# Feeding the first tile's raw weight pieces and the gated and last weights by converting transfers, with the raw copies moved beside the second layer's products

## The chip, the cores and the metric

The kernel runs on one core of a Trainium2 chip. The metric is device time in microseconds, lower is better. The profile shown is of one execution; the times are of three others.

## What is computed

The reference takes x of 8 x 1024 rows of 256 (8192 rows), normalises each row, and computes two things from it: a random-feature product `s` (256 features, exponentials, times a 256x256 matrix) and a ternary feed-forward net `g`. The output is `x + s * g`. Cut to the part that fills the time:

```python
h = silu(xn @ w1.T * w1_s) * (xn @ w2.T * w2_s)   # w1, w2: 1024 x 256, entries -1, 0, 1
h = gelu(h @ h1.T * h1_s)                          # h1: 1024 x 1024
h = gelu(h @ h2.T * h2_s)                          # h2: 1024 x 1024
g = silu(h @ w3.T * w3_s)                          # w3: 256 x 1024
out = x + s * g
```

## The kernel before

**Tiling.** T is 512 rows, a half; a tile is two halves, and there are NT = 8 tiles. A tile goes through: the gated layer (`gated`, `gated_step`, L331) for each half, the feature products (`dots`, `mix`), the two 1024x1024 layers (`product_layer`, L713), and the last layer (`down`, L780). Everything for TensorE is in fp32r. Each activation is split into a high and a low part (`split`, one conversion on ScalarE and one subtraction on VectorE), and each product is run for both parts.

**The fast scheme.** A 1024x1024 layer on a tile is a 2x2 block product done in seven products in place of eight (`FAST`, L32): with the raw weight blocks A11, A12 and A22 and with the sums S2, S1, S3 and S4 of blocks. The order in a layer is A11, A12, S2, S1, S3, S4, A22. Each of the seven is four groups m of 32/4 = 8 matmuls (four pieces k, high and low), so 32 matmuls; a layer is 224 matmuls on 28 pieces. A piece is 128x512 floats, 256 KB. Below, a product is numbered by w = 0 to 6 in its layer.

**The ring.** The pieces go through a ring of eight buffers (`RING`), in the order of `pieces` (L391), 56 a tile. `ring_step` (L416) waits for a piece, uses it, and at m = 3 marks the buffer free and calls `feed` (L397), which sends the piece eight places further on. So the four pieces of product w + 2 are sent while the last group of product w runs, and product w + 1 (32 matmuls) is the time they have to land. In the kernel before, the first eight pieces come straight from the weights by POOL's queue, which converts them to fp32r; all the others are sent by SP out of `hs`, a DRAM copy in which the raw blocks and the sums stand side by side, bit for bit. SP works through its waits and sends in the order written: a feed that waits for a sum to be stored holds all feeds behind it.

**The factory.** `factory` (L492) fills `hs`, on POOL. For each of eight (layer, k) it loads four raw blocks (two transfers of 512 KB, `load`), makes four sums with four tensor_tensor instructions (`make`), and stores them (1 MB). The buffers are borrowed from tiles that are needed later: `use` gives which, among them `quad[0]` (the third round), which VectorE must have back for its first sum t1, and F (`early`). `load(n)` waits until the last store out of its buffer has landed. Between its rounds the factory also sends `copy_raw` (L481), DRAM to DRAM copies of 1 MB that put a raw block of one layer into `hs`, six in all:

```python
            make(2)
            load(5)
            make(3)
            copy_raw(pool, 0, ["A22"])
            make(4)
            load(6)
            copy_raw(pool, 1, ["A11"])
```

`load(5)` stands ahead of `make(3)` and waits for the second round's store. After the factory POOL counts the weights' entries that are not -1, 0 or 1 (`count_good`, L551), with loads of 128 KB into `seen`; the count is read in the last tile.

**The start.** SP sends x of the first half, the column scales, proj, win, four transfers of w1 and w2 (halves, into `quad[1]` and `quad[4]`), x of the second half (L468 to L479). ScalarE converts w1 and w2 to fp32r (`round_w`, L590), for which matmuls of `gated_step` wait (`w12_ready`). The factory's first loads wait for all four w1/w2 transfers (L522).

**The norms.** `norms_out` (L314) stores 512 floats, one by one, from a 128x4 tile to DRAM (`q_h<-sm`); `norms_in` waits for them and reads them back as a row.

**w3.** It goes by SP from its array to a rearranged DRAM copy `w3d` (L897) and from there into `w3` (L932); `down` needs it at the end of the first tile.

**x of the next tile.** `load_x` for the next two halves stands between `dots` and `mix` (L900), ahead of SP's stores of s; their statistics are `fill` tasks in products 2 and 3 of the first layer.

Of the kernel before, what the change touches and what calls it, by code (L numbers as in the profile page):

```python
# [5 lines left out]
P = 128  # L6
D = 256
H = 1024
R = 256
T = 512  # L10
NB = T // P
KD = D // P
KH = H // P
Q = KH // 2
# [9 lines left out]
RING = 8  # L24
# [69 lines left out]
def build(nc, x, win, proj, cols_in, w3s_in, wT, out):  # L94
# [3 lines left out]
    with ExitStack() as ctx:  # L98
# [57 lines left out]
        q_h = nc.dram_tensor("q_h", [NH, NB, P], F32).ap()  # L156
        w3d = nc.dram_tensor("w3d", [P, KH * D], F32).ap()
        s_h = nc.dram_tensor("s_h", [NH, P, NB, D], F32).ap()
# [8 lines left out]
        def port(name):  # L167
            return Port(sem(name))
# [5 lines left out]
        d_first = [port(f"d_first{i}") for i in range(RING)]  # L174
        d_w3d = port("d_w3d")
        d_land = [port(f"d_land{i}") for i in range(5)]
# [18 lines left out]
        def cast(dst, src, *tokens, func=ACT.Identity, scale=1.0):  # L195
            act.wait(*tokens)
            return act.mark(lambda e: e.activation(dst, src, func, scale=scale))  # L197
# [48 lines left out]
        def load_x(h):  # L246
            sp.wait(*xin_free[h % 2])
            return d_x[h % 2].send(sp, xin[h % 2][:, :, :], x_h[h])
# [76 lines left out]

        w_round = {}

        def w12_ready(m):
            return [w_round[n, m // Q] for n in range(2)]

# [60 lines left out]
        pieces = [(layer, name, k) for _ in range(NT) for layer in range(2) for name, _ in FAST for k in range(Q)]  # L391
        fed = [0]
        ring_free = [[] for _ in range(RING)]
# [3 lines left out]
        def feed():  # L397
            n = fed[0]
            if n == len(pieces):
                return  # L400
            fed[0] += 1
            layer, name, k = pieces[n]
            p = PIECES.index(name)
            src = hs[layer][k][:, p, :]
            if n < RING:

                src = wT["h1"].rearrange("(j k p) (i c) -> j i k p c", j=2, p=P, i=2)[p // 2, p % 2, k]
                d_first[n].send(pool, ring[n][:, :], src)
                return
            sp.wait(piece_stored[layer, k, name if p < Q else "sums"])  # L410
            sp.wait(*ring_free[n % RING])
            d_ring[n % RING].send(sp, ring[n % RING][:, :].bitcast(F32), src)

        taken = [0]

        def ring_step(m, bank, slot, first, last, *tokens):  # L416

            pe.wait(*free[bank], *tokens)
            for k in range(Q):
                n = taken[0] + k  # L420
                i = n % RING
                pe.wait(d_first[i].token if n < RING else (d_ring[i].sem, 16 * (n // RING)))
                for g in range(2):
                    begins, ends = first and k == 0 and g == 0, last and k == Q - 1 and g == 1
                    args = ps[:, bank, :], ring[i][:, m * P:(m + 1) * P], slot[:, k, g, :], begins, ends, True
                    if g == 1 and (k == Q - 1 or m == Q - 1):
                        tok = mm_mark(*args)
                    else:
                        mm(*args)
                if m == Q - 1:  # L430
                    ring_free[i] = [tok]
                    feed()
            if m == Q - 1:
                taken[0] += Q
            return tok
# [35 lines left out]
        d_wi.send(sp, wi, win.rearrange("(a p) d -> p a d", p=P))  # L471
        lands = {}
        for half in range(2):
            for n, name in enumerate(("w1", "w2")):
                lands[n, half] = quad[(1, 4)[n]][:, 2 * half:2 * half + 2, :]
                d_w12[2 * n + half].send(sp, lands[n, half], w_kpm[name][:, :, half * T:(half + 1) * T])
        load_x(1)
# [14 lines left out]
        def factory():  # L492
# [28 lines left out]

            pool.wait(*(v.token for v in d_w12))  # L522
            for n in range(4):
# [6 lines left out]
            make(1)  # L530
            make(2)
            load(5)
            make(3)
            copy_raw(pool, 0, ["A22"])
            make(4)
            load(6)
            copy_raw(pool, 1, ["A11"])
            make(5)
            load(7)
            copy_raw(pool, 1, ["A12"])  # L540
            make(6)
            copy_raw(pool, 1, ["A22"])
            make(7)
            copy_raw(pool, 0, ["A11", "A12"])
            s_free[0][:] = s_free[1][:] = [stored[0].token]
# [42 lines left out]
        a_ab = act.mark(lambda e: e.activation(amp[:, 0, :], xis, ACT.Exp))  # L588

        def round_w(half):  # L590
            for n, w in enumerate((w1, w2)):
                w_round[n, half] = cast(w[:, :, half * T:(half + 1) * T], lands[n, half], d_w12[2 * n + half].token)

# [245 lines left out]
        rest_win = turn_win()  # L839
        round_w(0)  # L840
        for task in stats_tasks([0]):
# [5 lines left out]
        norms_win()  # L847
        round_w(1)
        quad_free[1] = quad_free[4] = [w_round[1, 1]]

# [3 lines left out]
        for t in range(NT):  # L854
# [40 lines left out]
            dots(h1, (6, 7), L0.at["v"])  # L895
            if t == 0:
                d_w3d.send(sp, w3d.rearrange("p (k d) -> p k d", k=KH), w_kpm["w3"])  # L897
                counted[0] = count_good()
            if t + 1 < NT:
                load_x(h0 + 2)  # L900
                load_x(h1 + 2)
                fills += stats_tasks([h0 + 2, h1 + 2])
            else:
                fills.append(count_odd)
                load_x(h0)

# [8 lines left out]
            if t:  # L915
# [4 lines left out]
            quad_free[L0.at["v"]] = [mix_done[h0], mix_done[h1]]  # L920

            product_layer(L0, L1, {
                (0, 0): [] if t else sums[:2], (0, 1): [] if t else sums[2:], (0, 2): [sub(L0, "t3", 0)], (0, 3): [sub(L0, "t3", 1)],
                (1, 0): [split(L0, "t2", 0)], (1, 1): [split(L0, "t2", 1)], (1, 2): [sub(L0, "t4", 0)], (1, 3): [sub(L0, "t4", 1)],
# [4 lines left out]
                (6, 0): [split(L1, "b11", 0)], (6, 1): [split(L1, "b11", 1)], (6, 2): [sub(L1, "t1", 0)], (6, 3): [sub(L1, "t1", 1)]})  # L929
            if t == 0:  # L930
                sp.wait(d_w3d.token)
                d_w3.send(sp, w3[:, :, :].rearrange("p k d -> p (k d)").bitcast(F32), w3d)  # L932
            product_layer(L1, C, {
                (0, 0): [split(L1, "b21", 0)], (0, 1): [split(L1, "b21", 1)], (0, 2): [sub(L1, "t2", 0)], (0, 3): [sub(L1, "t2", 1)],
# [4 lines left out]
                (5, 0): [split(L1, "t4", 0)], (5, 1): [split(L1, "t4", 1)], (5, 2): [fill, fill], (5, 3): [fill, fill],  # L939
                (6, 0): [split(C, "b22", 0, C.slot)], (6, 1): [split(C, "b22", 1, C.slot)], (6, 2): [fill, fill], (6, 3): [fill, fill, fill, fill, norms_away]})  # L940
            quad_free[C.at["b22"]] = [C.ready["b22"]]
# [180 lines left out]
```

How the kernel before makes its waits and increments, by code:

```python
    def wait(self, *tokens):  # L44
        for sem, value in tokens:
            if self.passed.get(id(sem), 0) < value:
                self.passed[id(sem)] = value
                self.todo.append(lambda e, s=sem, v=value: e.wait_ge(s, v))
# [4 lines left out]
    def mark(self, make):  # L53
        self.count += 1
        self.todo.append(lambda e: make(e).then_inc(self.sem, 1))
        return self.sem, self.count
# [9 lines left out]
    def play(self, engine, flag, ready):  # L66
        for make in self.always:
            make(engine)
        engine.wait_ge(*ready)
        value = engine.value_load(flag)
        for make in self.closing:
            make(engine)
        with engine.If(value > 0):
            for make in self.todo:
                make(engine)
# [8 lines left out]
    def send(self, lane, dst, src, **how):  # L84
        self.count += 16
        lane.todo.append(lambda e: e.dma_start(dst, src, **how).then_inc(self.sem, 16))
        return self.sem, self.count
```

## Time and profile before

| | us |
|---|---|
| median of 3 runs | 1333.66 |
| lowest, highest | 1329.79, 1334.7 |
| the profiled execution's own time | 1337.81 |
| its span in the trace | 1336.0 |
| TensorE (PE) busy | 1309.7 (98%) |
| VectorE (DVE) busy | 943.8 (71%) |
| ScalarE (ACT) busy | 759.1 (57%) |
| GpSimd (POOL) busy | 600.2 (45%) |

PE is TensorE's matmuls, PEld its weight loads, DVE VectorE, ACT ScalarE, POOL GpSimd, SP SyncE. Times in a view are microseconds from the start of the span; `x28` is a count; brackets hold the idle time before an instruction and what ended it. "us to landing" is the median from the issue of a DMA to its arrival. The SP and POOL queues of DMAs are called q1 hardware_dynamic and q0 software_dynamic. Matmuls overlap in the pipeline: 0.39 us each, one every 0.23 us.

### The profile page before, as it was taken

What the parts mean: (1) busy time and instruction counts of PE and PEld (TensorE: products, weight loads), DVE (VectorE), ACT (ScalarE), POOL (GpSimd) and SP (SyncE); (2) the same over time, 40 slices, a digit from 0 to 9 for tenths busy, and PEclk for the clock granted to TensorE, in tenths of its full rate; (3) what the DMA queues carried; (4) which work ended last, traced back from release to release, by engine and by line L of the source; (5) the groups of instructions that cost most, each with busy time, mean ns of one, the idle gap of its engine ahead of it and who ended that gap; (6) DMA issues with size and microseconds to landing.
All of it is one profiled execution on the core that took longest, in us unless ns stands there. A gap on an engine that the chain in (4) does not pass through costs nothing.

```text
span 1336.0 us, 16514 instructions
## 1 busy us (share of the span) xinstructions
PE 1309.7 (98%) x6300; PEld 1106.8 (83%) x6300; DVE 943.8 (71%) x1205; ACT 759.1 (57%) x1020; POOL 600.2 (45%) x606
## 2 busy tenths in 40 slices
PE   7988999999999999999999999999999999999998
PEld 6866898888988888888898888888888888988887
DVE  6595876788677786777876767657767577665665
ACT  5445555566455664556654666546565565655664
POOL 4695978999789996888877000000000000000000
PEclk9989999999999999999999999999999999999999
DMA  9998553454625454345452443514443244413441
GB/s 240 311 360 309 178 133 104 146 169 153 128 91 170 148 175 100 110 148 179 143 139 74 151 149 106 141 64 156 130 106 129 95 136 149 123 67 112 141 157 50
DMA packets 97556, 195.98 MB, mean 147 GB/s; under 512 B 19136, under 2 KB 21440, under 8 KB 96320
## 3 DMA queue, kind: packets, MB, share of 16 engines
q1 hardware_dynamic: 87008, 158.16, 37.9%
q0 software_dynamic: 10464, 36.71, 9.2%
q8 instruction: 52, 0.85, 0.3%
q14 instruction: 32, 0.26, 0.1%
HBM read 169.62 MB, written 32.54 MB: 151 GB/s over the span
## 4 chain that ended last, share of the span: by engine, by line
PE 88%; DMA 6%; DVE 3%; POOL 2%; ACT 1%; issue 1%; SPq 0%; POOLq 0%; DVEq 0%
PE ps L218 68%; PE ps L221 19%; DMA ring<-hs 2%; DVE quad L201 1%; DMA hs<-quad 1%; DMA s<-in_h 1%; DMA q_h<-sm 1%; PE ps L305 1%; DMA quad<-in_w 1%; DMA ry<-in_x 1%; POOL ry L510 1%; DVE split L201 1%; POOL quad L510 0%; POOL s L510 0%; DVE xin L207 0%
## 5 line engine op out<-in xcount | busy, mean ns | idle before, releaser
L218 PE MATMUL ps<-split,ring 128*128 128x512 f32 x2800 | 769.2, 391 | 11.4 <-DMA ring<-hs 6.2
L218 PEld LDWEIGHTS ps<-split,ring 128*128 128x128 f32 x2800 | 527.8, 189 | 124.4 <-DMA ring<-hs 9.4
L201 DVE TENSOR_TENSOR split<-quad,split 128x1024 fp32r<-128x1024 f32 x258 | 336.6, 1313 | 186.6 <-ACT split L197 185.6
L197 ACT ACTIVATE split<-quad 128x1024 fp32r<-128x1024 f32 x258 | 267.5, 1053 | 72.5 <-PE ps L221 70.4
L221 PE MATMUL ps<-split,ring 128*128 128x512 f32 x784 | 305.5, 390 | 0.0
L218 PE MATMUL ps<-xT,w 128*128 128x512 f32 x768 | 217.0, 391 | 0.8 <-DVE ry L201 0.7
L557 POOL TENSOR_TENSOR cube<-cube,seen 128x256 f32<-128x256 f32 x176 | 201.9, 1147 | 13.8
L197 ACT ACTIVATE quad<-ps 128x512 f32<-128x512 f32 x192 | 114.8, 598 | 138.4 <-PE ps L221 138.3
L197 ACT ACTIVATE quad<-quad,cols 128x512 f32<-128x512 f32 (+1 forms) x194 | 139.3, 720 | 87.6 <-DVE quad L201 87.0
L201 DVE TENSOR_TENSOR quad<-quad 128x1024 f32<-128x1024 f32 x128 | 179.5, 1443 | 7.8 <-DMA hs<-quad 7.8
L221 PEld LDWEIGHTS ps<-split,ring 128*128 128x128 f32 x784 | 147.4, 188 | 30.5
L218 PEld LDWEIGHTS ps<-xT,w 128*128 128x128 f32 x768 | 143.9, 189 | 31.0 <-DVE ry L201 1.1
L201 DVE TENSOR_TENSOR quad<-ps,quad 128x512 f32<-128x512 f32 x192 | 131.1, 685 | 35.5 <-ACT quad L197 25.5
L211 DVE SCALAR_TENSOR_TENSOR quad<-ps,cols,rows 128x512 f32<-128x512 f32 x128 | 94.3, 747 | 63.3 <-PE ps L221 49.1
L197 ACT ACTIVATE rows<-ps,cols 128x512 f32<-128x512 f32 x128 | 87.4, 689 | 83.5 <-PE ps L221 79.0
L568 POOL TENSOR_SCALAR cube<-cube 128x256 f32<-128x256 f32 x88 | 110.7, 1258 | 8.0
L221 PE MATMUL ps<-xT,w 128*128 128x512 f32 x256 | 99.9, 390 | 0.0
L557 POOL TENSOR_TENSOR good<-good,cube 128x256 f32<-128x256 f32 x88 | 90.1, 1024 | 7.3
L557 POOL TENSOR_TENSOR cube<-seen 128x256 f32<-128x256 f32 x88 | 69.6, 790 | 41.0 <-DMA seen<-in_h 33.8
L218 PE MATMUL ps<-w,split 128*128 128x256 f32 x476 | 66.3, 284 | 0.2 <-DVE split L201 0.2
L218 PEld LDWEIGHTS ps<-w,split 128*128 128x128 f32 x476 | 61.9, 191 | 0.4 <-DVE split L201 0.3
L197 ACT ACTIVATE quad<-ps,cols 128x512 f32<-128x512 f32 x64 | 43.0, 683 | 27.8 <-PE ps L221 27.7
(92 smaller groups left out, 1026.2 us busy)
## 6 DMA issues: line engine op xcount, KB each, us to landing
ring<-hs SPq DMA_DIRECT2D x440, 256.0 KB, 3.6
xin<-in_x SPq DMA_DIRECT2D x17, 512.0 KB, 5.6
s_h<-s SPq DMA_DIRECT2D x16, 512.0 KB, 2.6
seen<-in_h POOLq DMA_DIRECT2D x64, 128.0 KB, 3.7
ry<-in_x SPq DMA_DIRECT2D x15, 512.0 KB, 5.7
out<-ry SPq DMA_DIRECT2D x15, 512.0 KB, 2.9
hs<-in_h POOLq DMA_DIRECT2D x6, 1024.0 KB, 12.8
early<-in_h POOLq DMA_DIRECT2D x8, 512.0 KB, 15.7
```

What stands on the lines that cost most here:

```text
L197: return act.mark(lambda e: e.activation(dst, src, func, scale=scale))
L201: return dve.mark(lambda e: e.tensor_tensor(dst, a, b, op))
L211: return dve.mark(lambda e: e.scalar_tensor_tensor(out=dst, in0=a, scalar=scalar, in1=b, op0=op0, op1=op1))
L218: pe.run(lambda e: e.matmul(dst, stat, mov, start=start, stop=stop, skip_group_check=loose))
L221: return pe.mark(lambda e: e.matmul(dst, stat, mov, start=start, stop=stop, skip_group_check=loose))
L305: return e.transpose(ps[:, banks[kd], b * P:(b + 1) * P], xin[j][:, b, kd * P:(kd + 1) * P], ident[:, :])
L510: pool.wait(pool.mark(lambda e: e.tensor_tensor(dst, a, b, op)))
L557: pool.wait(pool.mark(lambda e: e.tensor_tensor(dst, a, b, op)))
L568: pool.wait(pool.mark(lambda e: e.tensor_scalar(cube[:, :], cube[:, :], 0.0, None, ALU.is_equal)))
```

## The change

- The factory's rounds: `make(1)`, `make(2)`, `make(3)` follow one another, with `load(5)` behind `make(3)`, and no copy between rounds; only layer 1's A22 is still copied by POOL, behind the last round.
- The first tile's raw pieces, except layer 1's A22, are sent by POOL straight from the weights and converted on the way: pieces 0 to 7 as before, 24 to 27 (layer 0's A22) and 28 to 35 (layer 1's A11, A12) new. They stand behind the factory on POOL, each behind a wait for its ring buffer.
- w1 and w2 are sent by POOL with conversion; ScalarE's `round_w` goes. The factory waits for the first halves only. w3 is sent by POOL with conversion, behind the factory; `w3d` goes.
- The five other raw copies are sent by SP, one ahead of each of the products 0 to 4 of layer 1 (in the job at m = 2) in the first tile.
- `count_good` stands behind the first layer. `load_x` for the next tile is a job at (0, 3) of the first layer, behind the stores of s.

```diff
@@ -323,10 +321,8 @@
-        w_round = {}
         def w12_ready(m):
-            return [w_round[n, m // Q] for n in range(2)]
+            return [d_w12[2 * n + m // Q].token for n in range(2)]
@@ -389,7 +385,7 @@
         pieces = [(layer, name, k) for _ in range(NT) for layer in range(2) for name, _ in FAST for k in range(Q)]
-        fed = [0]
+        fed, fed_by = [0], {}
         ring_free = [[] for _ in range(RING)]
@@ -402,14 +398,15 @@
             src = hs[layer][k][:, p, :]
-            if n < RING:
-                src = wT["h1"].rearrange("(j k p) (i c) -> j i k p c", j=2, p=P, i=2)[p // 2, p % 2, k]
-                d_first[n].send(pool, ring[n][:, :], src)
+            if n < 2 * len(FAST) * Q and p < Q and (layer, name) != (1, "A22"):
+                src = wT[("h1", "h2")[layer]].rearrange("(j k p) (i c) -> j i k p c", j=2, p=P, i=2)[p // 2, p % 2, k]
+                pool.wait(*ring_free[n % RING])
+                fed_by[n] = d_first[n % RING].send(pool, ring[n % RING][:, :], src)
                 return
             sp.wait(*ring_free[n % RING])
-            d_ring[n % RING].send(sp, ring[n % RING][:, :].bitcast(F32), src)
+            fed_by[n] = d_ring[n % RING].send(sp, ring[n % RING][:, :].bitcast(F32), src)
@@ -419,7 +416,7 @@
                 i = n % RING
-                pe.wait(d_first[i].token if n < RING else (d_ring[i].sem, 16 * (n // RING)))
+                pe.wait(fed_by[n])
                 for g in range(2):
@@ -469,11 +466,9 @@
         d_wi.send(sp, wi, win.rearrange("(a p) d -> p a d", p=P))
-        lands = {}
         for half in range(2):
-            for n, name in enumerate(("w1", "w2")):
-                lands[n, half] = quad[(1, 4)[n]][:, 2 * half:2 * half + 2, :]
-                d_w12[2 * n + half].send(sp, lands[n, half], w_kpm[name][:, :, half * T:(half + 1) * T])
+            for n, (name, w) in enumerate((("w1", w1), ("w2", w2))):
+                d_w12[2 * n + half].send(pool, w[:, :, half * T:(half + 1) * T], w_kpm[name][:, :, half * T:(half + 1) * T])
         load_x(1)
@@ -519,7 +514,7 @@
-            pool.wait(*(v.token for v in d_w12))
+            pool.wait(d_w12[0].token, d_w12[2].token)
             for n in range(4):
@@ -529,19 +524,16 @@
             make(2)
+            make(3)
             load(5)
-            make(3)
-            copy_raw(pool, 0, ["A22"])
             make(4)
             load(6)
-            copy_raw(pool, 1, ["A11"])
             make(5)
             load(7)
-            copy_raw(pool, 1, ["A12"])
             make(6)
+            make(7)
             copy_raw(pool, 1, ["A22"])
-            make(7)
-            copy_raw(pool, 0, ["A11", "A12"])
+            d_w3.send(pool, w3[:, :, :], w_kpm["w3"])
             s_free[0][:] = s_free[1][:] = [stored[0].token]
@@ -586,10 +578,6 @@
         a_ab = act.mark(lambda e: e.activation(amp[:, 0, :], xis, ACT.Exp))
-        def round_w(half):
-            for n, w in enumerate((w1, w2)):
-                w_round[n, half] = cast(w[:, :, half * T:(half + 1) * T], lands[n, half], d_w12[2 * n + half].token)
@@ -837,7 +825,6 @@
         rest_win = turn_win()
-        round_w(0)
         for task in stats_tasks([0]):
@@ -845,8 +832,6 @@
         norms_win()
-        round_w(1)
-        quad_free[1] = quad_free[4] = [w_round[1, 1]]
@@ -893,16 +878,10 @@
             dots(h1, (6, 7), L0.at["v"])
-            if t == 0:
-                d_w3d.send(sp, w3d.rearrange("p (k d) -> p k d", k=KH), w_kpm["w3"])
-                counted[0] = count_good()
             if t + 1 < NT:
-                load_x(h0 + 2)
-                load_x(h1 + 2)
                 fills += stats_tasks([h0 + 2, h1 + 2])
                 fills.append(count_odd)
-                load_x(h0)
@@ -919,25 +898,32 @@
+            def next_rows():
+                for h in (h0 + 2, h1 + 2) if t + 1 < NT else (h0,):
+                    load_x(h)
             product_layer(L0, L1, {
-                (0, 0): [] if t else sums[:2], (0, 1): [] if t else sums[2:], (0, 2): [sub(L0, "t3", 0)], (0, 3): [sub(L0, "t3", 1)],
+                (0, 0): [] if t else sums[:2], (0, 1): [] if t else sums[2:], (0, 2): [sub(L0, "t3", 0)], (0, 3): [sub(L0, "t3", 1), next_rows],
                 (1, 0): [split(L0, "t2", 0)], (1, 1): [split(L0, "t2", 1)], (1, 2): [sub(L0, "t4", 0)], (1, 3): [sub(L0, "t4", 1)],
                 (6, 0): [split(L1, "b11", 0)], (6, 1): [split(L1, "b11", 1)], (6, 2): [sub(L1, "t1", 0)], (6, 3): [sub(L1, "t1", 1)]})
-            if t == 0:
-                sp.wait(d_w3d.token)
-                d_w3.send(sp, w3[:, :, :].rearrange("p k d -> p (k d)").bitcast(F32), w3d)
-            product_layer(L1, C, {
+            jobs = {
                 (0, 0): [split(L1, "b21", 0)], (0, 1): [split(L1, "b21", 1)], (0, 2): [sub(L1, "t2", 0)], (0, 3): [sub(L1, "t2", 1)],
                 (5, 0): [split(L1, "t4", 0)], (5, 1): [split(L1, "t4", 1)], (5, 2): [fill, fill], (5, 3): [fill, fill],
-                (6, 0): [split(C, "b22", 0, C.slot)], (6, 1): [split(C, "b22", 1, C.slot)], (6, 2): [fill, fill], (6, 3): [fill, fill, fill, fill, norms_away]})
+                (6, 0): [split(C, "b22", 0, C.slot)], (6, 1): [split(C, "b22", 1, C.slot)], (6, 2): [fill, fill], (6, 3): [fill, fill, fill, fill, norms_away]}
+            if t == 0:
+                counted[0] = count_good()
+                for w, (layer, name) in enumerate(((0, "A11"), (0, "A12"), (0, "A22"), (1, "A11"), (1, "A12"))):
+                    jobs[w, 2] = jobs.get((w, 2), []) + [lambda layer=layer, name=name: copy_raw(sp, layer, [name])]
+            product_layer(L1, C, jobs)
             quad_free[C.at["b22"]] = [C.ready["b22"]]
```

## Rows read from the trace of the kernel before

**Rows 1.** Stretches, core 0: us, then PE, PEld, DVE, ACT, POOL busy, PEclk, DMA share, GB/s.

```profile
0.00:15.20 15.20, 7.44 (x32) 6.66 (x33) 9.91 (x39) 9.80 (x17) 3.02 (x12) 1.00 0.94 267
15.20:60.60 45.40, 45.33 (x205) 37.53 (x203) 27.14 (x54) 23.20 (x33) 28.40 (x32) 1.00 0.92 260
60.60:129.30 68.70, 57.28 (x227) 44.54 (x226) 51.95 (x62) 30.78 (x41) 50.61 (x45) 0.93 0.93 344
129.30:180.00 50.70, 50.70 (x225) 41.97 (x225) 43.18 (x43) 32.19 (x44) 46.03 (x44) 1.00 0.56 185
180.00:1300.00 1120.00, 1119.32 (x5429) 949.33 (x5428) 789.58 (x980) 644.54 (x864) 472.19 (x477) 1.00 0.43 129
1300.00:1336.00 36.00, 29.63 (x192) 26.81 (x190) 22.02 (x31) 18.62 (x25) 0.00 (x0) 0.98 0.19 70
```

**Rows 2.** Timeline of PE in the first tile's first layer.

```profile
80.50 3.33 PE L218 MATMUL ps<-split,ring 128*128 128x512 f32 x7 [5.04 <-ACT quad L197]
...
100.26 0.73 PE L218 MATMUL ps<-split,ring 128*128 128x512 f32 x2 [1.42 <-DMA ring<-hs]
102.09 0.56 PE L218 MATMUL ps<-split,ring 128*128 128x512 f32 x1 [1.10 <-DMA ring<-hs]
...
114.00 0.50 PE L218 MATMUL ps<-split,ring 128*128 128x512 f32 x1 [2.38 <-DMA ring<-hs]
...
123.10 0.50 PE L218 MATMUL ps<-split,ring 128*128 128x512 f32 x1 [0.88 <-DMA ring<-hs]
```

**Rows 3.** The chain that ended last, from 0 to 140: start us, us, what.

```profile
48.76 13.82 DMA hs<-quad
```

**Rows 4.** Timeline of DVE, 0 to 140: six sums in one merged row.

```profile
62.61 13.85 DVE L201 TENSOR_TENSOR quad<-quad 128x1024 f32<-128x1024 f32 x6 [7.79 <-DMA hs<-quad]
```

**Rows 5.** Timeline of POOL, 0 to 130.

```profile
26.75 5.39 POOL L510 TENSOR_TENSOR s<-s 128x512 f32<-128x512 f32 x4 [4.90 <-DMA s<-in_h]
...
59.82 1.06 POOL L86 DMA_DIRECT2D ry<-in_h  x2 [10.47 <-DMA hs<-ry]
...
68.33 0.58 POOL L86 DMA_DIRECT2D hs<-early  x1 [0.30 <-POOL early L510]
...
105.85 0.57 POOL L86 DMA_DIRECT2D hs<-early  x1 [0.30 <-POOL early L510]
```

**Rows 6.** DMA issues in the stretches 66 to 69 (two rows), 74 to 77, 95 to 99.

```profile
hs<-early POOLq DMA_DIRECT2D x1, 1024.0 KB, 6.6
...
ring<-hs SPq DMA_DIRECT2D x3, 256.0 KB, 4.1
...
ring<-hs SPq DMA_DIRECT2D x5, 256.0 KB, 5.2
...
ring<-hs SPq DMA_DIRECT2D x4, 256.0 KB, 13.7
```

**Rows 7.** Three other stretches, columns as in rows 1.

```profile
13.50:21.50 8.00, 8.00 (x35) 6.83 (x34) 4.74 (x19) 4.58 (x6) 8.00 (x16) 1.00 1.09 38
...
44.00:60.00 16.00, 16.00 (x74) 13.56 (x73) 5.06 (x8) 7.61 (x12) 5.00 (x6) 1.00 1.08 410
...
185.00:194.00 9.00, 9.00 (x79) 9.00 (x78) 4.24 (x5) 2.74 (x6) 6.13 (x8) 1.00 0.50 16
```

**Rows 8.** SP's queue of DMAs, 0 to 60.

```profile
10.35 0.38 SPq L86 DMA_DIRECT2D q_h<-sm  x1
21.17 0.32 SPq L86 DMA_DIRECT2D rows<-q_h  x1
...
44.07 0.67 SPq L86 DMA_DIRECT2D w3d<-in_w  x1
```

**Rows 9.** DMA issues over the whole span: KB each, us to landing.

```profile
ring<-hs SPq DMA_DIRECT2D x440, 256.0 KB, 3.6
...
seen<-in_h POOLq DMA_DIRECT2D x64, 128.0 KB, 3.7
...
hs<-in_h POOLq DMA_DIRECT2D x6, 1024.0 KB, 12.8
```

More of the change, by code:

```diff
@@ L156, in build @@
         q_h = nc.dram_tensor("q_h", [NH, NB, P], F32).ap()
-        w3d = nc.dram_tensor("w3d", [P, KH * D], F32).ap()
         s_h = nc.dram_tensor("s_h", [NH, P, NB, D], F32).ap()
@@ L174, in build @@
         d_first = [port(f"d_first{i}") for i in range(RING)]
-        d_w3d = port("d_w3d")
         d_land = [port(f"d_land{i}") for i in range(5)]
```

## Prediction

> **What bounds the kernel now.** I read the stretches first. TensorE is busy without a break from 180 to 1300 (1119.3 of 1120 us) and nearly so from 15.2 to 60.6; what is idle lies in the first 15 us, in the last 36, and in one stage between, the first tile's first layer [rows 1]. That stage and the next run the same 224 products: the second takes 50.7 us at full clock, the first 68.7. So the stage can give back at most 68.7 - 50.7 = 18.0 us. Of this 68.7 - 57.3 = 11.4 is idle; the other 6.6 are products at half clock behind a gap (the granted clock averages 0.93 here, 1.00 in the next stage) and short hitches.
>
> The timeline of TensorE then says which waits [rows 2]. There is one gap of 5.04 us ahead of product w = 2, and there are gaps of 2.5, 2.4 and, at w = 6, 0.9 us, where the ring's pieces are late (a fifth, of 0.4, stands beside the last). Seven matmuls behind the first gap take 3.33 us; elsewhere they take 1.75.
>
> The chain gives the first gap's cause [rows 3]: the factory's third store, issued at 48.8, lands only at 62.6. VectorE, idle for 7.79 us since 54.8, cannot take `quad[0]` back before; then it does six sums in 13.9 us [rows 4] and the splits that w = 2 needs. A second cause ends at nearly the same time: the fourth round is stored at 68.3 only [rows 5], lands 6.6 later, and the fourth piece of S2, fed after it, takes some 5.2 more [rows 6], to about 80.
>
> The late pieces have one cause. From 44 to 60 the DMA engines move 410 GB/s and are full [rows 7], and over the stage they are busy 93% at 344 GB/s, where the next has 56% [rows 1]. A piece takes 4.1 us to land at 67, 5.2 at 75, 13.7 at 96 [rows 6]. It may take 7.25: product w + 1, 32 matmuls of 50.7 / 224 = 0.226 us.
>
> **The change, part by part.** The sum is made against the profiled execution's own 1337.8, which is 4.1 above the median of 1333.7; I subtract the same gain from the median.
>
> *DMA bytes.* Five copies of 1 MB leave the stage, one stays, w3 is moved once, not twice, the first of its moves having stood at 44 [rows 8], and x of the next tile, which went right behind it, is sent after the stores of s. At 410 GB/s the 2 MB of w3 and x alone delay what is behind them on the engines by about 5 us between 44 and 62. The five copies are 5 x 2.6 = 13 us of engine time, between 69 and 121.
>
> *The first gap.* The third store then lands at about 62.6 - 5 = 57.5, and some 1 us sooner if the factory starts sooner (below). VectorE is free from 54.8, so its sums start at about 57 and not 62.6: 5.6 us, against a gap of 5.04. `make(3)` no longer stands behind `load(5)`, which waited 10.47 us [rows 5]: its store comes near 56 instead of 68.3, so the second cause goes altogether. Gain: 5.0 idle and an estimated 2.3 of slow products, less 0.3 that I leave. From below, if the store lands at 59.5: 3. I take 7.0. What is late next is VectorE: its sums take 2.3 us each here, beside a POOL that now computes without a pause.
>
> *Ring waits.* These hold the rest, 18.0 - 7.3 = 10.7. The factory's work between 26.8 and 105.9 [rows 5], 79 us, loses the 10.5 of waiting and some 2.4 of four copies' issues (at 0.6, as the store in the same rows); it ends near 90. From 56 to 89 it loads and stores 7 MB, then come 2 MB (A22's copy, w3). The ring asks 1 MB per 7.25 us, s and x are 2 MB: 7 + 4.6 + 2 = 13.6 MB in 33 us, 0.41 MB/us: just the engines' rate. So it is better than before but not free. For w = 2 to 4 I expect landings of 4 to 7 us; for w = 5, fed at 89 beside the factory's last 3 MB, about 10, a stall of up to 3. Bounds: all 10.7 back, or 4 of it if POOL's queue keeps a backlog. I take 7, a third left.
>
> *POOL's feeds.* Twelve pieces now wait on POOL, issued at about 0.6 us each behind the factory. The first, needed at 104, is sent when its buffer comes free at 95, by when the factory is over. Behind the waiting instruction stand only later feeds and the count, which is read in the last tile. Loads of 128 KB on this queue land in 3.7 us, the ring's pieces of 256 KB on SP's in 3.6 [rows 9]. Cost 0; if the factory ended 10 us late, a few us in w = 6.
>
> The Trainium skill, "SBUF — State Buffer", section "SBUF: two separate sides", speaks against this part: descriptors of DMAs issued by GpSimd are written through a port that VectorE can hold. [...]
>
> *Copies by SP.* Each is issued at the start of a product, behind the last feed, and has about 6 us before the next four feeds. At 2.6 us of engine time it is gone by then, and 2 MB per 7.25 us is 290 GB/s where 185 are used now [rows 1] and 410 have been reached. Cost 0. Below nothing is excluded, since TensorE has no idle time in that stage; above, see rival 3: the copies' median to landing is 12.8 us [rows 9], under full engines. I take the end nearer the engines' rate, since the stage has them half free.
>
> *The start.* ScalarE loses four conversions, 4.1 us, but the gated layer starts at 15.2 on TensorE's own products, so that gives 0. The w1 and w2 transfers now share the engines with x, proj and win instead of queueing behind them; x may land half a us later, and everything to 15.2 hangs on it: -0.5 (bounds +0.5, -6, rival 4). Their second halves can be caught by the first store of norms. While that is outstanding (issued 10.35, read back at 21.17 [rows 8]) the engines move 38 GB/s, and 16 in another such stretch, behind the next tile's stores at 182 [rows 7]. They would then land near 20, and are needed at 15.2 + 4 x 1.8 = 22.5: hidden, but if that cover goes they cost what they are late. The factory's first loads are issued by 10 instead of 13.2 but pass this same store; `make(0)` starts 1 to 3 us sooner.
>
> *x later, other tiles.* `load_x` has 2.25 products, 16 us, between its new place and its use, for 1 MB that takes 2.6 us of the engines: 0. After 180 there is nothing to gain or to lose but the last 36 us, untouched.
>
> Sum: 7.0 + 7.0 - 0.5 = 13.5. 1337.8 - 13.5 = 1324.3 for the profiled execution, 1333.7 - 13.5 = 1320 for the median.
>
> **Rivals.**
> 1. *The engines stay full.* The factory's rounds are closer together, and its traffic from 56 to 89 is as dense as it was from 68 to 99. If POOL's queue always has a backlog, a piece of SP's takes 10 us or more, as at 96 [rows 6], and w = 3, 4 and 5 each stall 3. For it: the balance of 0.41 above. Against it: the same density left 5.2 us at 75. Gain 4.5: 1329.
> 2. *POOL's transfers are late.* With 13.7 us to landing [rows 6] against 8.8 allowed, A22 of layer 0 and A11, A12 of layer 1 cost 4.9 each, 14.7 in all: no gain, 1335. Against it: by then the engines have room and the 3.7 of [rows 9] holds.
> 3. *The other side, slower: SP's copies hold the ring.* They stand in the queue of the ring's feeds. If a copy keeps that queue for its 12.8 us and four pieces take 3.6 more [rows 9], layer 1 gets its pieces every 16.4 us and needs them every 7.25: 5 x 9.2 - 7.3 of lead = 38 us, less the 13.5: 1358. It decides from the point where copy and four pieces together exceed 7.25 us. Against it: the engines are half idle there.
> 4. *First halves caught.* If w1's and w2's first halves are not in by 10.4, they wait for the norms' store and the gated layer starts at 21 instead of 15.2. TensorE then also meets a factory that is 6 us further on, so some comes back: 1325.
>
> **How the numbers follow.** My forecast 0.64; rival 1 0.16, rival 2 0.09, rival 3 0.05, rival 4 0.06. Own range of the forecast: gain 10 to 18, so 1316 to 1324. To leave out no more than 2 in 10 the range takes in rivals 4 and 1: 1315 to 1330. A change of 0.5%, 6.7 us, is about what a measurement of this kernel can tell from none. Faster by more: the forecast, rival 4 and a fifth of rival 1, 0.74. Within: the rest of rival 1 and most of rival 2, 0.20. Slower: rival 3 and the bad end of rival 2, 0.06.
>
> **What would show it.** The stage from the first ring product to the start of layer 1 shrinks from 68.7 to about 54. The sums on VectorE start near 57, with no gap ahead of w = 2. POOL's rounds 2, 3 and 4 stand without idle time, and the factory ends near 90. Ring pieces land in under 8 us except near 90. Layer 1 still takes 50.7. The gated layer starts at 15 to 16. It is wrong if layer 1 shows waits for ring pieces (rivals 2 and 3, told apart by which queue sent them), if gaps stay at w = 4 and 5 (rival 1), or if the first gated product waits for a transfer (rival 4).

## The result and the profile after

The changed kernel takes 1329.12 us (median of 20 runs, 1327.1 to 1333.03), the kernel before 1333.55 (20 runs, 1329.56 to 1336.7): a ratio of 0.9972, 95% interval 0.9963 to 0.9981. That is 4.4 us faster, inside the 0.5% that was called no change. The predicted 1320 asked for 13.5 us: a third of it came. In a later group of runs, where the kernel before took 1329.6, the ratio was 0.9992 (0.9982 to 1.0002).

The profiled execution's own time is 1328.22, its span 1326.4, against the 1336.0 of the span before. The stretches of the changed kernel, columns as in [rows 1]:

```profile
15.20:60.60 45.40, 45.35 (x206) 37.32 (x205) 31.92 (x55) 23.54 (x35) 37.26 (x39) 1.00 0.92 274
60.60:129.30 68.70, 60.77 (x260) 49.30 (x259) 54.32 (x66) 36.52 (x49) 44.45 (x43) 0.98 0.89 300
180.00:1300.00 1120.00, 1119.07 (x5389) 947.59 (x5389) 791.26 (x979) 645.51 (x865) 464.93 (x479) 1.00 0.43 130
```

The middle stretch has 60.8 us of work in TensorE where it had 57.3, since layer 1 starts inside it. A better measure is the one used below for every kernel: the time from the first ring product to the first product of `down`, less the 50.7 us of layer 1. I call it the first layer's stage. Before it was 119.3 - 50.7 = 68.6; after it is 170.2 - 58.3 - 50.7 = 61.2. So the two profiles differ by 7.4 in the stage and by 2.3 ahead of it (the first ring product at 58.3, not 60.6), together the 9.6 between the spans.

The timeline of TensorE in the changed kernel says what is left in the stage, against [rows 2]:

```profile
74.34 1.85 PE L216 MATMUL ps<-split,ring 128*128 128x512 f32 x7 [1.18 <-ACT quad L195]
84.22 1.89 PE L216 MATMUL ps<-split,ring 128*128 128x512 f32 x7 [2.35 <-DVE split L199]
110.67 3.25 PE L216 MATMUL ps<-split,ring 128*128 128x512 f32 x7 [4.39 <-DMA ring<-in_h]
```

The 5.04 us ahead of product 2 are 1.2. A gap of 2.4 is new ahead of product 3. The waits at products 4 and 5 are gone. At product 6 stands one of 4.4, with seven matmuls at half clock behind it (3.25 us instead of 1.75; the granted clock from 110.7 to 113.9 is 0.53). It waits for `ring<-in_h`: A22, one of the pieces that the change gave to POOL. The timeline of POOL's queue there:

```profile
56.25 1.06 POOL L86 DMA_DIRECT2D ry<-in_h  x2 [1.50 <-DMA hs<-ry]
...
93.66 0.58 POOL L86 DMA_DIRECT2D hs<-early  x1 [0.30 <-POOL early L505]
94.23 0.67 POOL L86 DMA_DIRECT2D hs<-in_h  x1
94.89 0.92 POOL L86 DMA_DIRECT2D w<-in_w  x1
97.96 2.14 POOL L86 DMA_DIRECT2D ring<-in_h  x4 [2.16 <-PE ps L219]
```

The wait of `load(5)` is 1.5 us where it was 10.5 [rows 5]. But three transfers of 1 MB, the last store, the last copy and w3, are sent within 5 us of the four pieces and stand ahead of them. What they take to land, with SP's feeds for product 5 from the same time, and the three groups of POOL's feeds in turn (DMA issues of 89 to 96, 97 to 101, 105 to 108, 113 to 121; us to landing last):

```profile
ring<-hs SPq DMA_DIRECT2D x4, 256.0 KB, 4.1
hs<-in_h SPq DMA_DIRECT2D x1, 1024.0 KB, 9.5
hs<-early POOLq DMA_DIRECT2D x1, 1024.0 KB, 11.0
hs<-in_h POOLq DMA_DIRECT2D x1, 1024.0 KB, 12.7
w<-in_w POOLq DMA_DIRECT2D x1, 1024.0 KB, 15.0
...
ring<-in_h POOLq DMA_DIRECT2D x4, 256.0 KB, 12.8
...
ring<-in_h POOLq DMA_DIRECT2D x4, 256.0 KB, 8.2
...
ring<-in_h POOLq DMA_DIRECT2D x4, 256.0 KB, 3.8
```

SP's pieces landed in 4.1 at 90, 13.7 at 96 before [rows 6]. POOL's first four took 12.8, of which 8 were free.

The row `hs<-in_h SPq` is the first of SP's five copies. It was meant for layer 1, but it is issued at 92.2, inside the first layer: SP has no feed to wait for between the last piece of S4, at 90, and the first sum of layer 1, since the twelve pieces between are POOL's. So one more MB was on the engines beside the four pieces. It stood there in `pieces_first` below too, where the four pieces landed in 6.7; no run takes it away.

### The profile page after: what moved, and what is told of

Its sections match the earlier page's. It is cut to its first block, busy times and chain, and to the rows that moved or that the text cites. A ratio compares the mean times of both kernels' runs of the same rounds, so it can differ in the third digit from the quotient of the medians.

```text
span 1326.4 us, 16508 instructions
## 1 busy us (share of the span) xinstructions
PE 1303.6 (98%) x6300; PEld 1103.4 (83%) x6300; DVE 944.5 (71%) x1205; ACT 754.2 (57%) x1016; POOL 598.7 (45%) x618
## 4 chain that ended last, share of the span: by engine, by line
PE 88%; DMA 5%; DVE 3%; POOL 2%; ACT 1%; issue 1%; SPq 0%; POOLq 0%; DVEq 0%
PE ps L216 68%; PE ps L219 19%; DVE quad L199 2%; DMA ring<-in_h 1%; DMA s<-in_h 1%; DMA q_h<-sm 1%; DVE split L199 1%; DMA hs<-quad 1%; PE ps L303 1%; DMA w<-in_w 1%; DMA ry<-in_x 1%; POOL ry L505 1%; POOL quad L505 0%; POOL s L505 0%; DVE xin L205 0%
## 5 line engine op out<-in xcount | busy, mean ns | idle before, releaser
L560 POOL TENSOR_SCALAR cube<-cube 128x256 f32<-128x256 f32 x88 | 108.0, 1227 | 8.0
L549 POOL TENSOR_TENSOR cube<-seen 128x256 f32<-128x256 f32 x88 | 66.7, 758 | 31.3 <-DMA seen<-in_h 22.7
## 6 DMA issues: line engine op xcount, KB each, us to landing
ring<-in_h POOLq DMA_DIRECT2D x20, 256.0 KB, 12.8
```

The costliest lines, as they stand in the source:

```text
L549: pool.wait(pool.mark(lambda e: e.tensor_tensor(dst, a, b, op)))
L560: pool.wait(pool.mark(lambda e: e.tensor_scalar(cube[:, :], cube[:, :], 0.0, None, ALU.is_equal)))
```

## The experiments

Each group stood on one chip, beside the kernel before; the changed kernel itself has one run in the first group, ten in the fourth and none in the second and third. That took 1334.3 and 1334.0 us in the first two groups and 1328.7 and 1329.6 in the third and fourth, so times are compared by ratio across groups. The stage and its gaps come from one profile each.

### First group: two repeats, the queue, the start

`before_again` and `after_again` are the two kernels as they are.

> The kernel before, once more, for a second profile. The first profiled execution took 1337.8 us where the median of 20 is 1333.6. Theory A (the profiled execution had worse waits than most): the first layer's stage, 68.7 us there, takes 64 to 66, or the gated layer starts nearer 13.5 than 15.2. Theory B (the profile was typical and the time lies outside the stages): stage 68 to 69 again, and the time again near 1337.

> The changed kernel, once more, for a second profile. Theory A (its first profile is typical: 1328.2 against a median of 1329.1): a stage of 61 us from the first ring product to layer 1, with gaps of about 1.5, 2.5 and 4.5 us ahead of products 2, 3 and 6. Theory B (the gap ahead of product 6 is chance): no gap there and a stage of 55 to 56.

The kernel before took 1333.6, with a stage of 65.4 us, and the gated layer started at 13.4. The changed kernel took 1329.2, with a stage of 61.2 and the gap at product 6 again (4.0 us). So the trace on which the prediction rests was of an execution 4 us slower than the median, and 3.2 of that was lost in this very stage: theory A. That of the changed kernel is typical for this chip, theory A again, though the gap at product 2 was 0.4 us here.

`pieces_first`:

```diff
-            copy_raw(pool, 1, ["A22"])
-            d_w3.send(pool, w3[:, :, :], w_kpm["w3"])
...
             if t == 0:
+                copy_raw(pool, 1, ["A22"])
+                d_w3.send(pool, w3[:, :, :], w_kpm["w3"])
                 counted[0] = count_good()
```

> The changed kernel with POOL's last copy (A22 of layer 1) and w3 sent behind the twelve raw pieces and not ahead of them. Theory A (the gap ahead of product 6 is the queue: 2 MB stand ahead of four pieces that are needed 8 us after they are sent): pieces 24 to 27 land in 5 to 8 us and not in 12.8, the gap of 4.5 us and the slow products behind it go, 5 to 6 us faster than the changed kernel, about 1323.5. Theory B (the converting transfers are slow in themselves beside VectorE's work, so that descriptors are written late): they land in 10 us or more all the same, and the time stays within 1.5 us of 1329.

1324.32 us, ratio 0.9933 (0.9909 to 0.9956): 10 us faster than before, theory A. Pieces 24 to 27 land in 6.7, the next eight in 3.7 and 4.2, and no gap stands at product 6. Its stage is 53.5 us. The DMA issues of 97 to 101:

```profile
ring<-in_h POOLq DMA_DIRECT2D x4, 256.0 KB, 6.7
```

So the converting transfers are not slow in themselves; what stood ahead of them was.

`gated_undone` puts back the four SP transfers of w1 and w2, the two calls of `round_w`, and the factory's wait for all four transfers:

> The changed kernel with w1 and w2 sent by SP and converted by ScalarE again, as in the kernel before. Theory A (the 2.3 us by which the gated layer started sooner in the profile are only the moment at which the clock rose): the same time as the changed kernel within 1 us, about 1329, and a start of the gated layer between 13.5 and 15.2 that follows the clock. Theory B (ScalarE's conversions, or the order of the transfers, held the start): slower by 2 us, 1331, and a start at 15.2 again.

1329.96, ratio 0.9961 (0.9946 to 0.9977), no slower than the changed kernel: theory A. The gated layer started at 15.0. Over the profiles of these two kernels and this one it started at 15.2, 13.4, 13.4 (before), 13.5, 15.1, 15.4 (after) and 15.0: the 2.3 us of the first pair of profiles are the execution's, not the change's.

### Second group: one part taken back, and two mechanisms

`rounds_undone` has `load(5)` ahead of `make(3)` again.

> The changed kernel with load(5) ahead of make(3) again: the factory's fourth round waits for the second round's store as before. Theory A (the order of the rounds matters little once w3 and x no longer stand in front, since that wait is only 1.5 us in the changed kernel's profile): within 1.5 us of the changed kernel, about 1330. Theory B (the order is what removed the first gap): the gap ahead of product 2 comes back with 3 us or more, about 1333.

1334.71, ratio 1.0006 (0.9992 to 1.0019): the whole gain is gone. Neither theory had the place right: the gap at product 2 is 1.9 us, and that at product 6 is 8.6. POOL and TensorE in this kernel:

```profile
57.47 1.06 POOL L86 DMA_DIRECT2D ry<-in_h  x2 [9.79 <-DMA hs<-ry]
...
103.80 0.58 POOL L86 DMA_DIRECT2D hs<-early  x1 [0.30 <-POOL early L505]
...
105.03 0.92 POOL L86 DMA_DIRECT2D w<-in_w  x1
105.93 4.28 POOL L86 DMA_DIRECT2D ring<-in_h  x8
```

```profile
117.32 3.33 PE L216 MATMUL ps<-split,ring 128*128 128x512 f32 x7 [8.57 <-DMA ring<-in_h]
```

The wait is 9.8 us even without w3's and x's bytes ahead of it; it moves the factory's end to 103.8, and A22 is sent 8 us later than in the changed kernel, 5 of them after its buffers had come free. In this profile the order of the rounds matters because the raw pieces stand behind the factory.

`copies_undone` puts the six copies back on POOL between the rounds and takes SP's jobs out.

> The changed kernel with all six raw copies on POOL between the factory's rounds again, as before; the twelve raw pieces, w3 and the rest stay. Theory A (the copies filled the engines and POOL's queue): SP's pieces land in over 10 us at product 3 or later, and POOL's pieces behind 3 to 5 MB, in over 15: slower than the kernel before or equal to it, 1333 to 1340. Theory B (the copies' bytes were not what delayed the ring): within 2 us of the changed kernel, 1327 to 1331.

1333.54, ratio 0.9998 (0.9987 to 1.0008): no gain either. SP's pieces fed at 64 to 68 land in 11.6, those at 72 to 76 in 14.0 (6.3 and 5.4 in the changed kernel), and TensorE waits at products 2, 4, 5 and 6. Theory A, at its lower end.

`quad_first`:

```diff
-            use = [0, 1, 2, 4, 3, 1, 4, 3]
+            use = [2, 0, 1, 4, 3, 1, 4, 3]
```

> The changed kernel with quad[0] as the buffer of the factory's first round (s second, ry third). Theory A (the gaps of 1.2 and 2.4 us ahead of products 2 and 3 are VectorE's, which starts its sums at 58.4 because the third round's store lands then): the sums start near 53, both gaps go, 3 to 4 us faster than the changed kernel, 1325 to 1326. Theory B (the gap ahead of product 3 is VectorE slowed by POOL's sums at any hour): the gap at 3 stays above 1.5 us and the gain is under 1.5 us.

1329.69, ratio 0.9970 (0.9959 to 0.9981): as the changed kernel. VectorE's sums start at 53.4 and the gap at product 3 is gone, but product 2 now waits 1.7 us for ring pieces, which take 9.1 to land, and the gap at product 6 stands at 3.3. Both theories missed: the two causes stand side by side, VectorE's at product 3 and the ring's at product 2.

`norm_rows` is `pieces_first` with the norms stored in 128 runs of four floats; the exponents of the features take the norms of other rows.

```diff
-            q_stored[h % 2] = d_qout[h % 2].send(sp, q_h[h].rearrange("b p -> p b"), ...
+            q_stored[h % 2] = d_qout[h % 2].send(sp, q_h[h].rearrange("b (c e) -> (b c) e", e=NB), ...
```

> The kernel pieces_first with the norms stored as 128 runs of 16 bytes in place of 512 runs of 4; the norms then stand in another order, so the features' exponents take the norms of other rows. Theory A (the 512 single writes hold the DMA engines for some 8 us each time): the store is read back 3 us after its issue and not 11, the factory's first loads land at 17 to 19 and not at 26, its last round ends near 88, the gaps ahead of products 2 and 3 go: 1 to 3 us faster than pieces_first, 1322. Theory B (the engines stand still there for another reason, as POOL writing its descriptors): the first load still lands at 25 to 27 and nothing moves.

1326.01, ratio 0.9948 (0.9932 to 0.9964), not faster than `pieces_first`, though what theory A said of the transfers came in the main. SP's queue, then the stretch that moved 38 GB/s before [rows 7]:

```profile
10.34 0.33 SPq L86 DMA_DIRECT2D q_h<-sm  x1
15.04 0.32 SPq L86 DMA_DIRECT2D rows<-q_h  x1
```

```profile
13.50:21.50 8.00, 8.00 (x35) 6.84 (x35) 3.80 (x12) 3.33 (x4) 8.00 (x15) 1.00 0.99 281
```

The store is read back after 4.7 us, not 11; the engines move 281 GB/s; `make(0)` starts at 20.8 and the last round is stored at 82.7. The stage is 51.1: nothing is lost in it. But the first ring product stands at 70.8, 10 us late. The profiled execution took 1330.0, 4 us over the median of the six (four took 1324.8 to 1326.2), so the usual delay is smaller than this. The timeline of TensorE, and groups of VectorE's instructions between 15 and 45 here and in `pieces_first`:

```profile
34.45 1.65 PE L216 MATMUL ps<-xT,w 128*128 128x512 f32 x3 [4.32 <-DVE quad L209]
```

```profile
L205 DVE TENSOR_SCALAR xin<-xin,mv,sm 128x256 f32<-128x256 f32 x4 | 5.7, 1469 | 0.0
L209 DVE SCALAR_TENSOR_TENSOR sm<-sm 128x4 f32<-128x4 f32 x7 | 5.7, 813 | 0.2
```

```profile
L205 DVE TENSOR_SCALAR xin<-xin,mv,sm 128x256 f32<-128x256 f32 x4 | 2.4, 652 | 0.0
L209 DVE SCALAR_TENSOR_TENSOR sm<-sm 128x4 f32<-128x4 f32 x7 | 2.1, 299 | 0.2
```

The factory's sums now run beside the second half's statistics, and a SCALAR_TENSOR_TENSOR on 128x4 floats takes 0.81 us on average, up to 1.7, where it takes 0.15 to 0.16 in the timeline before the sums begin. Behind the 4.32 us gap the granted clock is 0.50. In `pieces_first` the sums begin at 25.6, when these instructions are nearly done (0.30 on average): the slow store of norms, which holds up the factory's loads, had kept POOL away from them. The Trainium skill, "SBUF — State Buffer", section "SBUF: two separate sides", says that VectorE and GpSimd share a pair of ports as a lock that is held for a whole instruction, and counts among what takes it a VectorE instruction with two inputs in SBUF beside a GpSimd instruction that reads SBUF, as the small ones here have. The waits, up to 1.5 us beside sums of 1.3 to 1.4, agree in the main.

### Third group: parts alone

`bytes_only` is the kernel before with w3 sent by POOL behind the factory and `load_x` at (0, 3). `rounds_only` is the kernel before with `make(3)` ahead of `load(5)`.

> The kernel before with three edits alone: no w3d, w3 sent by POOL behind the factory, and x of the next tile behind the stores of s. Theory A (the 2 MB that they take off the engines between 44 and 62 delay the third round's store): VectorE's sums start at 57 to 59 and not at 62.6, but the fourth round still stands behind load(5), so the gap ahead of product 2 only shrinks to 1 to 3 us: 1330 to 1332. Theory B (these bytes were never in the way): sums at 61 or later and no gain, 1334.

> The kernel before with the order of the rounds alone: make(3) ahead of load(5), all copies where they were. Theory A (the order gives what it gave inside the change, some 5 us between rounds_undone and the changed kernel): about 1329 to 1331. Theory B (with the copies still between the rounds the engines stay full, and the time gained on POOL comes back as waits for the ring's pieces): 1332 to 1334, with landings over 10 us from product 3 on.

`bytes_only`: 1330.18 against 1328.68, ratio 1.0015 (1.0001 to 1.0029). Its sums start at 56.5, even sooner than theory A had it, and the first gap is nearly gone (0.2 us; the kernel before, where it takes 1328.5, has 2.0 there, see the fourth group), but SP's pieces sent between 64 and 92 land in 8.7 to 11.9 and TensorE waits at five products: no gain, theory A's cause with theory B's time. `rounds_only`: 1335.02, ratio 1.0054 (1.0037 to 1.0071), slower than no change at all. In its profile four waits of 1.1 to 1.4 us stand in product 2 alone:

```profile
76.38 0.70 PE L218 MATMUL ps<-split,ring 128*128 128x512 f32 x2 [1.41 <-DMA ring<-hs]
78.20 0.83 PE L218 MATMUL ps<-split,ring 128*128 128x512 f32 x2 [1.11 <-DMA ring<-hs]
80.21 1.22 PE L218 MATMUL ps<-split,ring 128*128 128x512 f32 x2 [1.18 <-DMA ring<-hs]
82.87 0.80 PE L218 MATMUL ps<-split,ring 128*128 128x512 f32 x1 [1.44 <-DMA ring<-hs]
...
102.86 1.22 PE L218 MATMUL ps<-split,ring 128*128 128x512 f32 x2 [2.60 <-DMA ring<-hs]
```

Pieces fed at 72 to 77 take 14.5 us to land. Theory B, and worse than it said: a faster factory brings its copies to the engines sooner and the ring pays. The order pays only with the copies elsewhere, the copies elsewhere only with the order. This joins runs of two chips: on the chip of the fourth group, where the kernel before is as fast as here, the two together gave 0.9992.

`w3_late` (w3 behind the raw pieces, the copy ahead) and `both_first` (`pieces_first` and `quad_first` together):

> The changed kernel with w3 alone behind the twelve raw pieces; the copy of A22 stays ahead of them. Theory A (the gap ahead of product 6 goes with the bytes in POOL's queue): pieces 24 to 27 land about 2.5 us sooner than 12.8, the gap shrinks from 4.4 to about 2, 1326 to 1327. Theory B (w3's 1 KB runs hold the queue longer than their bytes): the gap goes altogether, 1324.

> The kernel pieces_first with quad[0] as the buffer of the first round. Theory A (the ring's pieces for product 2 then wait where VectorE waited, as in quad_first): 1323.5 to 1325, no better than pieces_first. Theory B (the two edits add, the 0.7 us gaps ahead of products 2 and 3 go): 1322 to 1323.

`w3_late`: 1323.16, ratio 0.9959 (0.9943 to 0.9974). Its TensorE at product 6, and the DMA issues of 96 to 102:

```profile
107.41 2.41 PE L216 MATMUL ps<-split,ring 128*128 128x512 f32 x7 [1.24 <-DMA ring<-in_h]
```

```profile
ring<-in_h POOLq DMA_DIRECT2D x4, 256.0 KB, 9.6
```

The four pieces land in 9.6, the gap is 1.2 us. One MB less in front gives 3.2 us sooner, and both MB less, in `pieces_first`, 6.1: theory A's mechanism, with somewhat more than it said. `both_first`: 1320.93, ratio 0.9949 (0.9936 to 0.9963), stage 52.4. `pieces_first` did not stand in this group; the fourth compares them.

### Fourth group: four kernels side by side

> The kernel before, a third profile, beside the three others on one chip. Theory A (what the kernel before loses in the first layer's stage differs from execution to execution and from chip to chip, and the gain of the change with it): a stage between 60 and 69 us, and the time follows it one for one. Theory B (the times differ outside that stage): a stage of 65 to 69 whatever the time.

> The changed kernel, against the kernel before on the same chip. Theory A (its gaps at products 2, 3 and 6 stand whatever the chip, while those of the kernel before shrink on some): the gain is 4 to 5 us where the kernel before takes 1334, and 0 to 3 us where it takes 1329. Theory B (the change takes the same time off everywhere): 4 to 5 us in either case.

> The kernel pieces_first again, beside the changed kernel on the same chip. Theory A (the gap ahead of product 6 costs 5 to 6 us with the slow products behind it): 4.5 to 6 us faster than the changed kernel. Theory B (some of the difference of the first session was chance): 2 to 4 us.

> The kernel both_first again, beside pieces_first on the same chip. Theory A (quad[0] in the first round gives the ring's waits what it takes from VectorE's): within 1 us of pieces_first. Theory B (they add): 1 to 2.5 us faster than pieces_first.

| kernel | us | ratio to before | stage in its profile |
|---|---|---|---|
| before | 1329.63 | 1 | 61.5 (that run: 1328.5) |
| changed | 1328.64 | 0.9992 (0.9982 to 1.0002) | 57.0 (that run: 1327.7) |
| pieces_first | 1321.33 | 0.9928 (0.9910 to 0.9946) | 57.7 (that run: 1326.4) |
| both_first | 1321.73 | 0.9939 (0.9921 to 0.9957) | 51.5 |

The kernel before has now shown a stage of 68.6, 65.4 and 61.5 us at 1337.8, 1333.6 and 1328.5, while the stretch from 180 to 1300 is full in each: its losses differ from execution to execution, and most of the differences in time lie there, as theory A said. In the third profile its sums start at 58.7 and the first gap is 2.0 us. `pieces_first` is 7.3 us faster than the changed kernel here, more than either theory had, and 4.8 faster than that kernel's one run in the first group; `both_first` is level with it, as theory A said, though its profile has the cleanest stage.

In this group's profile of the changed kernel there is no gap at product 6. Its ring started at 62.4, not 58.3, product 2 then waited 3.1 for SP's pieces, and POOL, whose last MB was sent at 92.3, was by then far ahead:

```profile
103.19 2.14 POOL L86 DMA_DIRECT2D ring<-in_h  x4 [10.03 <-PE ps L219]
```

The four pieces landed in 7.8 us, by 111, and product 6 began at 112. So theory A had the gain right (none to 3 us where the kernel before takes 1329), but not its reason: the gaps do not stand whatever the chip, and the waits stand in for one another. It also means that the 7.3 us of `pieces_first` in this group can't be read off these profiles: the one of the changed kernel shows no loss at product 6, and that of `pieces_first` is of an execution 5 us over its median, with 3.6 us of waits at product 2. Where the time went there stays open, and so does why the kernel before is faster in the third and fourth groups.

## Why the prediction was wrong

**The trace and the median.** The prediction's first step, a stage of 68.7 that can give back 18.0, was read off an execution 4.1 us above the median, and the same gain was then subtracted from the median. Most of the excess was lost in that stage (65.4 and 61.5 in two other profiles), so the median had about 14 to give, and 11 where the kernel before is at 1329. Of the 9.6 us between the two profiles, 4.3 are the first execution's, 0.9 the second's: 9.6 - 4.3 - 0.9 = 4.4. These 5.2 are more than half of the 9.1 us by which the prediction missed. The other 3.9 are the sum's: the stage still loses 10.5 us, 5.9 of it at product 6 and 3.8 at products 2 and 3, where the sum left 4.0 in all; against that the ring started 2.3 us sooner and not 0.5 later.

**The ring's waits: the step of the sum that failed most.** It had two halves. SP's pieces did what it said and better: they landed in 6.3, 5.4, 4.8 and 4.1 us, and the stall kept for product 5 did not come. (In the fourth group's profile product 2 did wait 3.1 us for them.) "POOL's feeds: cost 0" was wrong: 4.4 us of gap and 1.5 of slow products. The prediction had A22's copy and w3 in its byte count and charged them to SP's feeds, which share only the engines; it did not ask what stands in POOL's own queue ahead of four pieces needed 8 us after they are sent. It looked at when POOL is done issuing, not at when its queue is empty, and the factory ended at 94, not 90, its last rounds taking 7 to 8 us each. Nor did it see that SP's first copy would go at 92. `pieces_first` and `w3_late` show it: with 2, 1 and 0 MB of copy and w3 ahead the four pieces land in 12.8, 9.6 and 6.7 us and the gap is 4.4, 1.2 and nothing. `pieces_first`, with the same bytes in another order, has a stage of 53.5 us, where the prediction wrote about 54, and 0.9933. (In the fourth group's profile of the changed kernel this step cost nothing.)

**The first gap.** Gain expected 7.0, 0.3 left. The third store landed at 58.4, not 57, product 2 still waited 1.2, and VectorE, late since then, made product 3 wait 2.4: some 3.8 left, 3.5 gained. "What is late next is VectorE" named it, with no price.

**Rivals.** The measured 1329 is the time that rival 1 was given, and it lies inside the outer range of 1315 to 1330. That is luck: rival 1's stalls at products 3, 4 and 5 are not in the trace. Rival 2 had the right queue at too high a price: 12.8 us to land for the first four pieces, but 8.2 and 3.8 for the others, so one product waited and not three. POOL's pieces land in 3.7 to 4.2 with an empty queue, beside VectorE's splits. The Trainium skill, "SBUF — State Buffer", section "SBUF: two separate sides", has VectorE hold up the descriptors of GpSimd's DMAs in its 2-port modes, and says that `tensor_tensor` has none. The sums and splits here are `TENSOR_TENSOR`, so the rule that the prediction cites does not speak against its part, and these landings agree with the page but do not test the rule. `rounds_only` shows what rival 1 looks like. Rival 3 did not come: SP's copies took 6.8 to 9.5, the feeds behind them 3.7 to 5.5, and layer 1 had no gap. Of rival 4 the condition came and the consequence did not: the first halves of w1 and w2 were in at 12.5 and not by 10.4, yet they did not wait for the norms' store, and the gated layer started at 13.5, 1 us behind them.

**The start.** -0.5 was expected; nothing was measured beyond what executions of one kernel differ by. The factory's first loads were issued at 13.05, not by 10, and its first sums started at 25.9, not 26.8: 0.9 us sooner, where the prediction had 1 to 3.

**The parts.** The prediction added them. They do not add: without the order of the rounds 1.0006, without the moved copies 0.9998, where all together give 0.9972; the order alone 1.0054 and the bytes alone 1.0015, on a chip where the kernel before takes 1329; all together gave 0.9992 on another such chip.

## What to carry to other kernels

When a transfer with a deadline moves to another queue, list what that queue has been given and not yet landed at the moment of issue: here two transfers of 1 MB took four pieces from 6.7 to 12.8 us, and sending them after the pieces went with 5 us less on one chip and 7 on another, where the profiles don't show how. Before a ceiling is read off one trace, compare its own time with the median: what it is above is likely to be stalls in the very stage that one means to mend. And a producer that is made faster sends its bytes sooner; if the engines are full there, take bytes away in the same edit.

## What was not expected of the hardware

While a store of 512 single floats to DRAM (2 KB) is outstanding, the DMA engines move 38 to 62 GB/s for some 8 us, and it is read back 11 us after its issue; as 128 runs of 16 bytes it takes 4.7 and the engines move 281 GB/s beside it. Taking such a stall away can cost more than it gives: POOL's sums then ran beside VectorE's small instructions, which took up to ten times as long (1.7 us against 0.16), and in the one profile, of an execution 4 us over the median, the start of the ring moved from 61 to 71 us.
